# Projection of a decoder layer: the roots of four chunks' variances from VectorE to Pool, and moments a chunk sooner

## What is computed

```
def _layernorm(x, axis=-1, eps=1e-05):
    m = jnp.mean(x, axis=axis, keepdims=True)
    v = jnp.var(x, axis=axis, keepdims=True)
    return (x - m) / jnp.sqrt(v + eps)
...
        qkv = x @ qkv_w.T + qkv_b
        qkv = qkv.reshape(B, L, 3, H, D).transpose(2, 0, 3, 1, 4)
        q, k, v = (qkv[0], qkv[1], qkv[2])
        cos, sin = rope_cos_sin(L, D)
        q = apply_rotary(q, cos, sin)
        k = apply_rotary(k, cos, sin)
...
    x = x + _L0_attn_ref(_layernorm(x, axis=-1), L0_attn_qkv_w, L0_attn_qkv_b, L0_attn_proj_w, L0_attn_proj_b)
```

## Time and profile before

| what | value |
|---|---|
| median of 3 runs (lowest, highest) | 1166.14 us (1165.2, 1168.48) |
| profiled execution: its own time | 1170.64 us |
| its span, first to last instruction | 1168.9 us |
| busy share: PE, DVE, ACT, POOL | 91%, 86%, 66%, 46% |
| mean granted clock of PE over the span | 0.947 |
| projection: last DVE instruction starts | 99.65 us |
| first matmul of the attention block starts | 104.73 us |

### The profile page before, as it was taken

One profiled execution on the slowest core, in us unless ns is written; L12 is line 12 of the kernel. 1 busy time (PEld: TensorE's weight loads), 2 busy tenths in 40 slices (PEclk: granted clock), 3 DMA queues, 4 the chain that ended last, 5 costly groups with the idle time before them and its releaser, 6 DMA issues. The chain is left out here.

```text
span 1168.9 us, 23162 instructions
## 1 busy us (share of the span) xinstructions
PE 1066.8 (91%) x8508; PEld 593.9 (51%) x8508; DVE 1009.0 (86%) x2108; ACT 767.8 (66%) x932; POOL 533.4 (46%) x866
## 2 busy tenths in 40 slices
PE   7988899999999999999999999988883069999998
PEld 6875433333333333333333333357773048888897
DVE  8998999999999999999999999437998975666653
ACT  4551288888888888888888888944555024555653
POOL 2647945454545363545444523232200023766665
PEclk8998599999999999999999999989997559999999
DMA  6787743232322334242424220055522022554443
GB/s 236 260 250 216 173 80 80 49 74 50 77 56 63 62 64 70 46 78 50 84 39 85 48 54 16 21 153 175 191 84 95 0 87 70 145 144 115 113 113 36
DMA packets 90140, 114.03 MB, mean 98 GB/s; under 512 B 31104, under 2 KB 62832, under 8 KB 90032
## 3 DMA queue, kind: packets, MB, share of 16 engines
q1 hardware_dynamic: 66872, 69.57, 20.5%
q0 software_dynamic: 19824, 36.48, 15.8%
q10 hardware_dynamic: 3336, 6.56, 1.6%
HBM read 73.31 MB, written 38.27 MB: 95 GB/s over the span
## 5 line engine op out<-in xcount | busy, mean ns | idle before, releaser
L835 DVE TENSOR_REDUCE b_max_halves<-banks 128x1 f32<-128x512 f32 x1024 | 625.1, 681 | 7.5 <-PE banks L882 7.5
L760 ACT ACTIVATE b_probs<-banks 128x1024 f32<-128x1024 f32 x512 | 520.4, 1027 | 110.8 <-PE banks L913 110.8
L882 PE MATMUL banks<-b_k,b_q 62*128 62x512 f32 x1024 | 391.9, 467 | 12.3 <-DVE b_max_halves L835 4.5
L913 PE MATMUL banks<-b_q,b_k 64*128 64x512 f32 x1024 | 378.8, 453 | 0.1
L898 PE MATMUL banks<-b_probs,b_v 128*17 128x256 f32 (+1 forms) x3840 | 314.3, 400 | 0.2 <-ACT b_probs L760 0.2
L913 PEld LDWEIGHTS banks<-b_q,b_k 64*128 64x128 f32 x1024 | 158.2, 185 | 228.6 <-issue 180.6
L882 PEld LDWEIGHTS banks<-b_k,b_q 62*128 62x128 f32 x1024 | 164.0, 189 | 38.3 <-DVE b_max_halves L835 33.6
L898 PEld LDWEIGHTS banks<-b_probs,b_v 128*17 128x17 f32 x3840 | 63.9, 95 | 164.8 <-issue 96.9
L572 POOL TENSOR_TENSOR b_att<-b_out,b_rec_spread 128x512 f32<-128x512 f32 x32 | 40.8, 1276 | 165.6 <-DMA b_rec_spread<-reciprocals 127.3
L1613 POOL DMA_INDIRECT e_x<-rows,d_idx x32 | 45.3, 1416 | 110.3 <-DVE d_wx L1788 56.8
L1833 DVE TENSOR_TENSOR e_hTl<-e_hT,e_hTh 128x512 fp32r<-128x512 f32 x64 | 47.8, 746 | 48.3 <-ACT e_hT L1587 48.3
(11 more groups left out here) (264 smaller groups left out, 1586.7 us busy)
## 6 DMA issues: line engine op xcount, KB each, us to landing
e_w<-in_w SPq DMA_DIRECT2D x16, 1024.0 KB, 7.6
q_stacks<-a_parts SPq DMA_DIRECT2D x32, 256.0 KB, 3.9
k_stacks<-a_parts SPq DMA_DIRECT2D x32, 256.0 KB, 4.2
b_q<-q_stacks POOLq DMA_DIRECT2D x60, 128.0 KB, 3.4
b_k<-k_stacks POOLq DMA_DIRECT2D x30, 256.0 KB, 4.9
v_tiles<-a_v ACTq DMA_DIRECT2D x8, 544.0 KB, 3.6
b_rec_spread<-reciprocals SPq DMA_DIRECT2D x128, 32.0 KB, 4.4
attended<-b_att SPq DMA_DIRECT2D x128, 32.0 KB, 2.4
```

The costliest lines, as they stand in the source:

```text
L760: nc.scalar.activation(pr[:, S % NP, u], ps[:, 2 * u:2 * u + 2, :], ACT.Exp, scale=D ** -0.5).then_inc(s_ex[u], 1)
L835: v.tensor_reduce(mxp[:, (k // NB) % 2, s, p, t, kh:kh + 1], ps[:, bank(k), :], AX.X, ALU.max)\
L882: nc.tensor.matmul(ps[:, bank(k), :], qs[g][stack, h, p, P * t:P * t + P], ks[g][stack, p, CH * kh:CH * kh + CH], start=True, stop=True).t ...
L913: return nc.tensor.matmul(ps[:, 2 * u + s, :], ks[g][stack, u, P * kt:P * kt + P], qs[g][stack, h, u, :], start=True, stop=True)
```

## The change

DVE keeps the roots of chunks 0 to 3 and drops two groups, of chunks 4 and 5 and of 6 and 7. Pool makes them in `roots`, 16 dependent instructions for two chunks: written with `tensor_scalar` and `tensor_tensor` alone, so that a Newton step takes four instructions and not three. They stand at the head of Pool's turns n = 3 and n = 7, ahead of the clearing of `b_k` and of sum 3, and ahead of sum 7. The first waits until DVE has the moments of both chunks (`moments_at`) and until the chunks whose places in `rs` and `nm` are taken have been normalised. ACT's waits follow. So that both chunks' moments are there, DVE makes those of chunks 4 and 5 in chunk 1, of chunk 6 in chunk 2, of chunk 7 in chunk 3, and none in chunk 4.

```diff
--- before.py
+++ after.py
@@ -141,6 +141,8 @@
         s_pb = sem("a_trailing_part")
         s_v0 = s_bvb = sem("a_v_filled_then_its_bias_spread_then_multiplied")
         s_dch = sem("a_dve_step")
+        moments_at = {}
+        ROOT_STEPS = 16
 
         block = ctx.enter_context(nc.Block())
 
@@ -232,7 +234,7 @@
         def _(act):
             def normalise(c):
                 h = c % 2
-                act.wait_ge(s_stat, c + 1 if c < 2 else 2 + c // 2)
+                act.wait_ge(s_stat, c + 1 if c < 2 else 3 + ROOT_STEPS * (c // 2 - 1))
                 after(act, s_xT, c - 1)
                 for t in range(NT):
                     last = nc.scalar.activation(xn[:, h, t, :], xin[:, c % NX, t, :], ACT.Identity,
@@ -305,6 +307,7 @@
                 for t in range(NT):
                     ins = v.bn_aggr(mv[:, c % NX, t, :], st[:, h, t, :])
                 chain(ins)
+                moments_at[c] = chain.n
 
             def spread(c, n, between=None):
 
@@ -355,12 +358,14 @@
                     moments(3)
                 if c + 1 < J:
                     trailing(c + 1)
-                if c and c + 3 < J:
-                    moments(c + 3)
+                if c == 1:
+                    moments(4)
+                if c and c + 4 < J:
+                    moments(c + 4)
                 if 0 < c < J - 1:
                     split(2 * c - 1)
-                if c % 2 == 0 and c + 2 < J:
-                    spread(c + 2, 2)
+                if c == 0:
+                    spread(2, 2)
                 if c == 3:
                     for k in range(KC):
                         last = v.tensor_copy(bvb[:, k, :], bv[:, k:k + 1].to_broadcast([P, P]))
@@ -375,9 +380,30 @@
         @block.gpsimd
         def _(pool):
             g = nc.gpsimd
+            step = Chain(pool, s_stat, 3)
+
+            def roots(c):
+
+                u = slice(c % NX, c % NX + 2)
+                pool.wait_ge(s_dch, moments_at[c + 1])
+                if step.n == 0:
+                    pool.wait_ge(s_stat, 3)
+                pool.wait_ge(s_xn, c - NX + 2)
+                step(g.tensor_scalar(ve[:, u], mv[:, u, :, 1], 1.0, EPS, ALU.mult, ALU.add))
+                step(g.tensor_scalar(rs[:, u].bitcast(I32), ve[:, u].bitcast(I32), -0.5, MAGIC, ALU.mult, ALU.add))
+                for _ in range(3):
+                    step(g.tensor_tensor(tm[:, u], rs[:, u], rs[:, u], ALU.mult))
+                    step(g.tensor_tensor(tm[:, u], tm[:, u], ve[:, u], ALU.mult))
+                    step(g.tensor_scalar(tm[:, u], tm[:, u], -0.5, 1.5, ALU.mult, ALU.add))
+                    step(g.tensor_tensor(rs[:, u], rs[:, u], tm[:, u], ALU.mult))
+                step(g.tensor_scalar(tm[:, u], mv[:, u, :, 0], -1.0, 0.0, ALU.mult, ALU.add))
+                step(g.tensor_tensor(nm[:, u], tm[:, u], rs[:, u], ALU.mult))
+
             clear_pad(g, pool, group0[0], s_clear0, 0)
             for n in range(2 * J - 1):
                 q = n % 2
+                if n in (3, 7):
+                    roots((4, 6)[n // 4])
                 after(pool, s_eo, n)
                 if n == 3:
                     clear_pad(g, pool, group0[1], s_clear0, 2)
```

## The result

The kernel before ran at 1167.55 us median (1165.2 to 1170.92, 16 runs) and the changed one at 1173.59 us (1172.08 to 1178.27, 16 runs). The ratio is 1.0055, with a 95% interval of 1.0045 to 1.0065: **the change costs 6.4 us** (0.0055 x 1167.55; by the interval 5.3 to 7.6). Forecast were + 4.7 us and 1170.8 us, with a range that ended at 1173.5. The sign was right, the size was not, and the time lies 0.1 us over the range. Of the 2.8 us between 1170.8 and 1173.59, 1.4 are the base (1166.14 in the runs shown ahead, 1167.55 here) and the rest is the change's own; on the first base 6.4 us more would have been 1172.6, inside the range.

A forecast was written before the change was run, and what follows sets the result against it. The prediction took DVE to bound the middle and SP's issues after subtraction 7 the projection's end: 5.7 us later, less SP's idle 1.05, gives + 4.7 us. It forecast 1170.8 us, range 1166.8 to 1173.5.

The forecast's parts named there:

- The walk over DVE and Pool: Step-by-step timing of both engines through sums 3 and 7: DVE's end + 3.2 us, subtraction 7 + 5.7 us.
- the stall at subtraction 3: On DVE, waiting behind Pool's first roots, the clearing of b_k and sums 3 and 4: 5.2 us.
- at subtraction 7: DVE's stall behind Pool's second roots and sums 7 and 8: 3.05 us, some 1.25 of it even with sum 7 in time.
- subtraction 7 itself: Its end on DVE, from which SP's chain to the projection's end was counted: 76.5 and not 70.78 us, + 5.7.
- DVE's end: End of DVE's work in the projection: + 3.2 us, at 104.1, counting only if it gets past SP's end.
- A pitch of 0.29 us: Spacing of the 16 dependent root steps on Pool, 4.65 us in all; bounds 0.21 and 0.31 us.
- SP's idle 1.05 us: SP's pause waiting for subtraction 9, 81.76 to 82.81 us, would go and take 1.05 us off the lateness at SP's end.
- rival 2: SP's store issues after subtraction 7 shorten and DVE's end decides: + 0.1 to + 3 us; chance 0.08.
- 1: Pool's small root steps pass beside DVE's subtractions without waiting for the port: SP + 1.0 us, 1167.1 us; chance 0.20.
- 3: Pool's steps are hidden, pitch under 0.14 us with the port: faster, SP's end - 1.9 us, 1164.2 us; chance 0.10.
- 4: TensorE's lower clock after idling outlasts the cover in chunks 6 and 7, or steps take 0.35 us: + 6 to + 8 us; chance 0.10.
- The estimate of 0.39 us a step: Pool's root steps at twice DVE's own pitch of 0.19 us: + 8.0 us in place of + 4.7.

The follow-up runs named there:

- x2: The changed kernel with b_k's pad cleared at Pool's start, not between the first roots and sum 3; ratio to the kernel before 1.0031.
- x10: x2's kernel profiled once more, a single run: attention opens 2.9 us later than in the kernel before, stretch after subtraction 7 35.08 us.
- x4: The kernel before with one more 544 KB store, issued by ACT in chunk 5; ratio to the kernel before 1.0023.
- x7: The kernel before with the loads of the attention's first group in chunks 2 to 4, not 3 to 5; ratio to the kernel before 0.9981.
- x11: The changed kernel a third time, a single run: attention opens 6.4 us later than in the kernel before, stretch after subtraction 7 34.74 us.
- x9: The changed kernel run once more, unaltered; ratio to the kernel before 1.0061, stretch after subtraction 7 35.70 us.
- x3: The changed kernel with the second group of roots back on DVE, only the first on Pool; ratio to the kernel before 1.0032.

## Why the prediction was wrong: right over DVE and Pool, wrong at the block's end

**The walk over DVE and Pool held.** Forecast and measured: 5.2 and 4.93 us for the stall at subtraction 3 (49.09 to 54.02); 3.05 and 2.81 us at subtraction 7 (73.03 to 75.84); subtraction 7 itself + 5.7 and + 5.6; DVE's end + 3.2 and + 3.1, both from subtraction 0 on. The close match of the last two is in part luck: both stalls were put 0.25 us too long, and 0.32 us that DVE waited for TensorE's transposes (at 60.32) were put at nothing. A pitch of 0.29 us was taken for the steps and 0.28 came (39.27 to 39.55), of which 0.20 is the instruction, inside the bounds of 0.21 and 0.31. The port was taken to stop the chain for 1.0 us at each L340; the two steps that met one took 1.23 and 1.17 us and not 0.20, each of them until the L343 of 37.90 or 41.43 had ended. Clearing b_k took 3.66.

**The step that failed is the sum:** "SP's idle 1.05 us goes, since subtraction 9 is only 3.2 us late: 5.7 - 1.05 = + 4.7 us at SP's end". The pause went and the microsecond did not come: the term of - 1.05 measured nothing at the opening in the change, and nothing in x2 and x10. The prediction took SP's timeline for the resource and its issues for work of fixed length. But the same four stores, of sum 9, took SP 3.90 us in before, 4.58 in x4 and 4.95 in the change, and the DMA engines ran at a share of 0.95 through the stretch, 0.95 also around the pause. The sum had to be: end of subtraction 7, plus a stretch that is not shortened: + 5.6 us. x4 (0.557 MB more with SP's list unchanged, + 2.3 us) and x2 (no pause, opening late by what subtraction 7 is) show this; x7 (loads gone from the stretch, - 2.5 us) agrees, but it also took issues from SP. The prediction did say that the issues vary, but used that for rival 2 alone. It did not look at what the attention's first instructions wait for: beside the drains it is the landing of a load, `b_v<-v_tiles`, which in before comes at about the time of SP's drain (99.04 + 5.2 = 104.2, against 104.1).

**What is left,** some 0.8 us of the 6.4 (in the profiled executions + 6.4, + 6.9 and + 7.3 against + 5.6, so 0.8 to 1.7), is a stretch longer than before's, which the prediction took as unchanged. The interval of the times, 5.3 to 7.6 us, does not tell it from nothing; the profiles do. In the first 8 us behind subtraction 7 the DMA engines idle 1.0 us more than in before (shares of 0.70 and 0.80 against 0.82 and 0.93), but that does not decide it: x2 idles there as much (0.71 and 0.75) and has a stretch of 34.09. What goes with it in every execution is the order of the last store of v and the load of `b_v` (at x10 and x11). The load's own time from issue to landing varies too:

DMA issues of before and of the changed kernel (out<-in, engine, times, KB, us from issue to landing):
```profile
b_v<-v_tiles SPq DMA_DIRECT2D x1, 272.0 KB, 5.2
```
```profile
b_v<-v_tiles SPq DMA_DIRECT2D x1, 272.0 KB, 6.0
```
In x9, which has the longest of these eight stretches, it took 7.2 us; but in x3, which has the shortest, 6.5, and in x11 5.5. What sets this in one execution and not in another wasn't tried, and with a scatter of 1 us the cause of these 0.8 us stays open.

**The rivals.** 1 fell: steps of 8 numbers a partition do wait for the port. 2 was right in that SP's issues give: in x2 and x3 SP's drain comes 0.4 and 0.7 us sooner behind subtraction 7 than in before. But the opening doesn't follow, since the load it waits for doesn't land sooner, and in the change itself the chain grew, from 33.35 to 34.7 us. 3 fell with the pitch of 0.28. Of 4, the condition came at one of the two places and the price didn't: TensorE was idle 6.92 us ahead of chunk 4's transposes and was granted the lower level, 1.2 GHz, from that idle time on until 60 us, but the products were there almost in time. Ahead of chunk 6's transposes it was idle 1.28 us and not 7, its clock stayed at 1.00, and they took 1.09 us (at 79.00) and not 1.97 as in before. Timeline and windows of PE in the changed kernel, the latter with busy time, clock, DMA share and GB/s:
```profile
57.19 1.97 PE L431 MATMUL banks<-ident,a_xn 128*128 128x128 f32 x8 [6.92 <-ACT a_xn L240]
...
56.00:58.00 2.00, 0.81 (x4) 0.50 1.02 378
58.00:60.00 2.00, 2.00 (x9) 0.50 0.99 331
60.00:62.00 2.00, 2.00 (x9) 0.82 1.00 320
```
The time lies in the rival's region (+ 6 to + 8 us) for another reason than the rival's.

The estimate of 0.39 us a step from the Trainium skill ("GPSIMD Engine Reference", section 3) was too high here: the measured pitch is 0.28 us, against DVE's 0.19. What the Trainium skill says of the port ("SBUF — State Buffer", section "SBUF: two separate sides") holds for the smallest instructions too: 1.23 us for one whose neighbours take 0.20.

## What to carry to other kernels

A queue-issuing engine that is busy to the end is not yet the bound: read the DMA share of the same stretch. Here it stayed at 0.95 through the engine's pause, the pause was no slack, and what helped was to start transfers sooner, until ACT's end was the next bound. Before moving work to an engine with little to do, look at what stands behind it in that engine's list (here a clearing of 3.66 us and then a sum that DVE waits for) and not at its busy share. Here work on the other side paid: the loads of the next stage, started a chunk sooner, gave 2.2 us where taking 5 us of work off DVE, which had no gap, lost 6.4.

## What the runs showed of the hardware

- A Pool step of 128x8 with one input (L392, a multiplication and an addition of constants) waits for a two-input DVE instruction of 128x1024 as a sum of 128x1024 does: 1.23 us against 0.20.
- Dependent Pool steps of 128x8 stand 0.28 us apart, 0.08 of it between one's end and the next one's start; DVE's 13 of the same size stood 0.19 us apart.
- The issue of the same four stores of 256 KB on SP (those of sum 9) took 3.90 us in before and 4.58 us when ACT issued one more store of 544 KB among them, at 83.00 (x4).
- While the DMA engines' share of busy time was 0.95 to 0.97, they moved from 225 GB/s (the change, from 83.9 us on) to 307 GB/s (before, from 81 us on): the share and the rate are two things.
- A block's drains are not the whole of its end: the first matmul of the next follows SP's drain by 0.6 us in before, and by 1.2 us in x4 (105.2, 106.36) and 1.8 us in x9 (108.4, 110.21), where it waits for the load of `b_v` to land. 272 KB took 5.2 us from issue to landing in before, 7.2 us in x9.
